# Token scatter inside the feed-forward phase, with the first weights loaded ahead of the wait

## The reference, cut to what matters

```python
x = x + _L0_ffn_ref(_layernorm(x)[None], ...)   # capacity: top 936 tokens by a score, one MLP (256 -> 1024 -> 256), gelu
x = x + _L1_ffn_ref(_layernorm(x)[None], ...)   # switch: each token to 1 of 8 experts (256 -> 1024 -> 256), relu
x = x + _L2_ffn_ref(_layernorm(x)[None], ...)   # top-2 of 8 experts, per-expert affine of the normed token, gelu
x = x + _L3_ffn_ref(_layernorm(x)[None], ...)   # top-2 of 16 experts (256 -> 512 -> 256), relu, residual, layernorm
...
buf = zeros(E, C, D).at[idx, pos_safe].set(x)   # tokens are put beside the others of their expert
y = relu(buf @ w1 + b1) @ w2 + b2               # one expert's weights for its tokens
out = gate * y[idx, pos]                        # and taken back by the token
```

## Time and profile before

| what | value |
|---|---|
| median of 3 runs | 4655.58 us (4652.52 to 4660.18) |
| profiled execution, its own time | 4685.71 us |
| span of that execution, first to last instruction | 4684.1 us |
| busy: PE, DVE, POOL, ACT | 2923.7, 2212.2, 1871.3, 867.9 us |
| mean granted TensorE clock | 0.778 |
| DMA, mean over the span | 128 GB/s |

### The profile page before, as it was taken

The page is one execution under the profiler, slowest core; times in us unless marked ns, Lnnn a source line. Parts: engine busy times, 40 slices in busy tenths (PEclk is TensorE's granted clock), DMA queues, the critical chain, the costliest instruction groups (busy, mean ns, idle before and its releaser), DMA issues. The chain is left out here.

```text
span 4684.1 us, 57224 instructions
## 1 busy us (share of the span) xinstructions
PE 2923.7 (62%) x16851; PEld 2401.0 (51%) x16852; DVE 2212.2 (47%) x5663; ACT 867.9 (19%) x2228; POOL 1871.3 (40%) x1982
## 2 busy tenths in 40 slices
PE   3566746664666566642568626665949639947392
PEld 3455535553555355522556413335938639936382
DVE  6655645554555555564243437681064421134113
ACT  1122312221222122210112100001300103310020
POOL 4366546664666466624323467731010020020212
PEclk7788878777887778875678657676979859978696
DMA  6633323332333233303312133315947449945594
GB/s 157 217 89 89 78 65 89 88 83 59 89 90 88 57 87 89 89 15 124 100 55 74 28 82 93 92 41 190 304 145 240 150 159 328 325 150 174 181 333 128
DMA packets 357397, 598.97 MB, mean 128 GB/s; under 512 B 81862, under 2 KB 239864, under 8 KB 354808
## 3 DMA queue, kind: packets, MB, share of 16 engines
q1 hardware_dynamic: 245816, 357.76, 23.3%
q0 software_dynamic: 88640, 214.25, 16.3%
q10 hardware_dynamic: 22656, 23.54, 1.5%
HBM read 499.63 MB, written 95.75 MB: 127 GB/s over the span
## 5 line engine op out<-in xcount | busy, mean ns | idle before, releaser
L833 POOL DMA_INDIRECT gine_got<-gine_table,src x1056 | 1024.5, 970 | 619.7 <-issue 251.1
L893 PE MATMUL gine_p_sum<-gine_hot,gine_got 128*128 128x128 f32 x4224 | 846.2, 334 | 565.1 <-DVE stack_acc L930 200.1
L893 PEld LDWEIGHTS gine_p_sum<-gine_hot,gine_got 128*128 128x128 f32 x4224 | 707.4, 238 | 719.0 <-issue 648.6
L922 DVE TENSOR_TENSOR gine_got<-gine_got,gine_p_edge 128x256 f32<-128x256 f32 x1056 | 440.2, 418 | 633.5 <-PE gine_p_edge L884 365.0
L901 ACT ACTIVATE gine_got<-gine_got 128x256 f32<-128x256 f32 x1056 | 439.0, 417 | 1201.1 <-issue 750.5
L488 POOL DMA_INDIRECT adjacency<-value,place x264 | 281.1, 1065 | 475.9 <-POOLq L54 166.2
L930 DVE TENSOR_TENSOR stack_acc<-stack_acc,gine_p_sum 128x256 f32 x1056 | 438.9, 416 | 3.5 <-issue 0.7
L883 PE MATMUL gine_p_edge<-gine_w_a,edge_space 128*128 128x256 bf16 x1056 | 338.3, 320 | 42.6 <-issue 34.7
L1368 PE MATMUL ffn_p_h<-ffn_xt,ffn_w 128*128 128x128 f32 x2864 | 347.3, 279 | 1.1 <-DMA ffn_w<-in_L_ffn_w 0.7
L1368 PEld LDWEIGHTS ffn_p_h<-ffn_xt,ffn_w 128*128 128x128 f32 x2864 | 337.3, 196 | 3.8 <-DMA ffn_w<-in_L_ffn_w 2.6
L884 PE MATMUL gine_p_edge<-gine_w_b,edge_space 128*128 128x256 bf16 x1056 | 336.8, 319 | 0.0
(11 more groups left out here) (398 smaller groups left out, 3526.2 us busy)
## 6 DMA issues: line engine op xcount, KB each, us to landing
gcn_a<-adjacency SPq DMA_DIRECT2D x270, 320.0 KB
ffn_w<-in_L_ffn_W SPq DMA_DIRECT2D x74, 1024.0 KB
ffn_w<-in_L_ffn_w SPq DMA_DIRECT2D x60, 1024.0 KB
ffn_w<-in_L_ffn_w SPq DMA_DIRECT2D x90, 512.0 KB
adjacency<-zero_row ACTq DMA_DIRECT2D x3, 7200.0 KB, 43.8
gine_got<-gine_table,src POOLq DMA_INDIRECT x1056
h_table<-score_rows SPq DMA_DIRECT2D x15, 1056.0 KB
adjacency<-zero_row SPq DMA_DIRECT2D x1, 7200.0 KB, 28.1
```

The lines of the kernel that those rows point to most:

```text
L833: pool.indirect_dma_start(got[:, c % RING, :], None, table, bass.IndirectOffsetOnAxis(ap=rows[:, c:c + 1], axis=0)).then_inc(gathered[c % ...
L893: ins = nc.tensor.matmul(p_sum[d % 4][:, half * P:(half + 1) * P], got[:, d % RING, half * P:(half + 1) * P], hot[:, d % HOTS, :], start=T ...
L922: nc.vector.tensor_tensor(got[:, c % RING, :], got[:, c % RING, :], p_edge[c % 4][:, 0:D], ALU.add).then_inc(summed, 1)
```

## The change

The phase `spread` is gone. Its scatters are now the first instructions of POOL in the block of `expert_blocks`, on a semaphore `placed`. SP issues w1(0), the vectors, w2(0) and w1(1), then waits for `placed`, and then issues x(0), x(1) and x(2). After that its loop goes on as before, without the loads that are already issued. The four callers pass the tokens (`rows`) in.

```diff
-def scatter_tokens(nc, g, rows, r, slots):
-    with Phase(nc, "spread") as ph:
-        sent = ph.sem("sent")
-        block = ph.block()
-        @block.gpsimd
-        def _(pool):
-            for k in range(r.choices):
-                for t in range(T):
-                    pool.indirect_dma_start(slots, bass.IndirectOffsetOnAxis(ap=r.slot[:, k, t:t + 1], axis=0),
-                                            rows[:, t, :], None).then_inc(sent, 16)
-            pool.wait_ge(sent, 16 * r.choices * T)
-
-def expert_blocks(nc, g, slots, results, r, w1, b1, w2, b2, func, affine=None):
+def expert_blocks(nc, g, rows, slots, results, r, w1, b1, w2, b2, func, affine=None):
...
-        small_in = ph.sem("small_in")
+        small_in, placed = ph.sem("small_in"), ph.sem("placed")
...
-            load_x(0)
             load_w1(0)
             sp.dma_start(b1_sb[:, :, :], b1.rearrange("a p m -> p a m")).then_inc(small_in, 16)
             sp.dma_start(b2_sb[:, :, :].rearrange("p a n -> p (a n)"), row(b2.rearrange("a n -> (a n)"))).then_inc(small_in, 16)
             if affine is not None:
                 for k in range(2):
                     sp.dma_start(aff[:, k, :, :], affine[k].rearrange("a p m -> p a m")).then_inc(small_in, 16)
-            for n in range(1, 3):
+            load_w2(0)
+            load_w1(1)
+            sp.wait_ge(placed, 16 * r.choices * T)
+            for n in range(3):
                 load_x(n)
             for n in range(1, nb + 1):
-                if n < nb:
+                if 1 < n < nb:
                     load_w1(n)
                 if n + 2 < nb:
                     load_x(n + 2)
-                load_w2(n - 1)
+                if n > 1:
+                    load_w2(n - 1)

         @block.gpsimd
         def _(pool):
+            for k in range(r.choices):
+                for t in range(T):
+                    pool.indirect_dma_start(slots, bass.IndirectOffsetOnAxis(ap=r.slot[:, k, t:t + 1], axis=0),
+                                            rows[:, t, :], None).then_inc(placed, 16)
             for n in range(nb):
                 pool.wait_ge(y_ready, n + 1)
...
-        scatter_tokens(nc, g, xn, r, slots)
-        expert_blocks(nc, g, slots, results, r, ...)
+        expert_blocks(nc, g, xn, slots, results, r, ...)
```

More of the change, by code:

```diff
@@ L1501, in capacity_ffn @@
         rank_tokens(nc, g, xn, i["L0_ffn_wr"].rearrange("d o -> (d o)"), i["L0_ffn_br"], chosen, r)
-        scatter_tokens(nc, g, xn, r, slots)
-        expert_blocks(nc, g, slots, results, r, i["L0_ffn_w1"].rearrange("(a d) f -> a d f", a=1), i["L0_ffn_b1"],
+        expert_blocks(nc, g, xn, slots, results, r, i["L0_ffn_w1"].rearrange("(a d) f -> a d f", a=1), i["L0_ffn_b1"],
                       i["L0_ffn_w2"].rearrange("(a d) f -> a d f", a=1), i["L0_ffn_b2"].rearrange("(a d) -> a d", a=1),
@@ L1523, in switch_ffn @@
         choose_experts(nc, g, xt, i["L1_ffn_gate_w"], i["L1_ffn_gate_b"], r, slots, capacity=capacity)
-        scatter_tokens(nc, g, xn, r, slots)
-        expert_blocks(nc, g, slots, results, r, i["L1_ffn_w1"], i["L1_ffn_b1"], i["L1_ffn_w2"], i["L1_ffn_b2"], ACT.Relu)
+        expert_blocks(nc, g, xn, slots, results, r, i["L1_ffn_w1"], i["L1_ffn_b1"], i["L1_ffn_w2"], i["L1_ffn_b2"], ACT.Relu)
         combine(nc, g, results, r.slot, r, g.X, guard=True)
@@ L1538, in top2_gelu_ffn @@
         layernorm(nc, g, xn, xn)
-        scatter_tokens(nc, g, xn, r, slots)
-        expert_blocks(nc, g, slots, results, r, i["L2_ffn_W1"], i["L2_ffn_b1"], i["L2_ffn_W2"], i["L2_ffn_b2"], ACT.Gelu,
+        expert_blocks(nc, g, xn, slots, results, r, i["L2_ffn_W1"], i["L2_ffn_b1"], i["L2_ffn_W2"], i["L2_ffn_b2"], ACT.Gelu,
                       affine=(i["L2_ffn_ln_g"], i["L2_ffn_ln_b"]))
@@ L1553, in top2_relu_ffn @@
         choose_experts(nc, g, xt, i["L3_ffn_gate_w"], i["L3_ffn_gate_b"], r, slots)
-        scatter_tokens(nc, g, xn, r, slots)
-        expert_blocks(nc, g, slots, results, r, i["L3_ffn_w1"], i["L3_ffn_b1"], i["L3_ffn_w2"], i["L3_ffn_b2"], ACT.Relu)
+        expert_blocks(nc, g, xn, slots, results, r, i["L3_ffn_w1"], i["L3_ffn_b1"], i["L3_ffn_w2"], i["L3_ffn_b2"], ACT.Relu)
         combine(nc, g, results, r.slot, r, xn)
```

## The result

| kernel | median | range, runs | ratio to before |
|---|---|---|---|
| before | 4655.0 us | 4652.52 to 4660.18, 6 | |
| after | 4621.18 us | 4618.93 to 4625.39, 6 | 0.9926 [0.9913, 0.9939] |

The change saves 34.4 us, [28, 40]; the forecast was 36.3 us and 4619.3 us. The profiled execution of after took 4619.35 us with a span of 4617.7 us and a mean granted clock of 0.779. Lines have moved: the scatter is L1337, x L1300, w1 L1306, w2 L1312, b1 L1315, b2 L1316, the affine vectors L1319, `turn` L1352, `up` L1360, `take` L1409 (with the affine L1412), the store L1341, the gather L1445.

The account below looks back on a forecast made before the run. POOL's own pace was taken to bound the scatter stretch, leaving only the wait behind it: 57.3 us before less 21.0 after saves 36.3, from the median 4655.6 to 4619.3 us. Own range 4613 to 4630, overall 4611 to 4633.

Parts of the forecast that it names:

- the chain: From the last scatter's end to `up`(0)'s start: 57.3 us over four places before, 21.0 after.
- x(0) to `up`(0): From x(0)'s issue to the first `up`: 8.2, 10.2, 11.6 and 12.5 us before, 3.4 after, 3.6 in `top2`.
- The landing of a scatter: From the last scatter's end to x(0)'s issue after the change: 1.8 us in all four places.
- the 1.2 us more with 30 scatters: Longer wait before x(0) in `top2` and `moe`, counted as part of the phase change, not of the landing.
- The loads are hidden: Early weights and vectors, 4.2 MB in `switch`, are done before the last scatter lands; nothing taken for them.
- the forecast's two cases: `switch`'s early loads: 13.5 us at 312 GB/s, or 18.0 us at 235 GB/s, a tie but still no loss.
- Rival A: Weight loads delay scatter landing and x(0): 11.2 us lost in all, 25.1 saved, 4630.5 us; chance 0.10.
- Rival C: POOL's scatters stall beside weight traffic, 3.93 us more each; three per place give 4666.5 us; chance 0.04.
- Rival B: Only the barrier between scatters and loads goes, the start-up stays: 7.6 us saved, 4648.0 us; chance 0.06.
- `up`(0): First `up` in each place: same times as before, 6.34, 5.13, 6.37 and 3.54 us.
- so the rest is shifted whole: From the end of `up`(0) on, same full buffers and same order in both kernels, so no further gain or loss.
- The barrier term: Barrier between last scatter and x(0) removed: 1.3, 1.3, 2.5 and 2.5 us, 7.6 saved in all.

Follow-up runs that it names:

- e2: The changed kernel with w2(0) and w1(1) issued behind x(0) to x(2), only w1(0) and the vectors ahead of the wait; 4334.48 us, ratio 0.9923 to before.
- e3: The changed kernel with the vectors b1, b2 and the affine issued behind x(0) to x(2), the weights still early; 4349.86 us, ratio 0.9971 to before.
- e4: The changed kernel with three more loads of 1 MB each ahead of SP's wait in each place; 4347.23 us, ratio 0.9957 to before.
- e1: The changed kernel with SP waiting for the scatters before its first load, then loading in the order of before; 4364.44 us against 4363.07, ratio 1.0006.
- e7: The changed kernel with 30 matmuls of no use on PE before turn(0), started at the sixth-last scatter's landing; 4649.9 us, ratio 0.9934 to before.
- e6: The kernel before with one scatter phase for each choice, so two phases of 15 scatters in `top2` and `moe`; 4664.45 us, run once.
- e5: The changed kernel with one POOL drain right behind its scatters; 4621.14 us, ratio 0.9922 to before.
- the change again: The changed kernel itself, unedited, run again as the base for other runs beside it; 4623.73 us, ratio 0.9930 to before.
- e9: The changed kernel without POOL's drain at the end of the four feed-forward blocks; 4617.55 us, ratio 0.9912 to before.
- e11: The changed kernel with POOL drains behind the scatters and each result store, none at the feed-forward blocks' ends; 4668.09 us, ratio 0.9967 to before.

## Why the prediction was right, and where not

- **What bounds the stretch.** Right. POOL's pace sets the scatter stretch (1.28 us, as before), and the only thing to be had was the chain behind it. e2 and e3 show the chain's parts one by one.
- **x(0) to `up`(0).** Forecast 3.4 us and 3.6 in `top2`; measured 3.44 to 3.50, and 3.74. This term carries the result: 28.5 of the 37.6 us. By e3 18.6 of them are the vectors.
- **The landing of a scatter.** Forecast 1.8 us from a gather's wait; 1.43 measured, in all four places. It was good for 1.5 us more than forecast. Right too was that the 1.2 us more with 30 scatters were not landing.
- **The loads are hidden.** Right, with DMA at 0.9 in the scatter stretch. In `switch` they took 17.4 us from SP's first issue and were done 1.7 us before the last scatter ended. That is near the worse of the forecast's two cases, 13.5 and 18.0, not the one it went by: 4.2 MB in 17.4 us are 241 GB/s, not 312. It was made good in part by the start, 0.25 us before the first scatter where the forecast had 0.8 after it. Rival A did not happen, but in `switch` it is near. e4 shows what it is like: SP waits 3.6 and 3.4 us more, nearly all of it for the scatters' own data. Rival A's price, 3.2 us for one weight load, was not measured: e4 adds three.
- **Rival C.** No scatter's instruction stalled: 1.02 us at most in after, and the pace held in e4 beside full DMA engines. But the instruction is not the whole scatter: in e4 the data came 3 us late at an unchanged pace, which the argument from the 539 ns of a store could not see.
- **Rival B.** e1 is this rival built: only the barrier goes. The forecast gave it 7.6 us; it saved nothing that the medians show.
- **`up`(0).** The sum was forecast unchanged at 21.4 and is 20.9, with single ones off by up to 1.5 us either way. e7 shows that the clock at 0.50 is what makes them long.
- **The step that failed** is "so the rest is shifted whole". The forecast put the 1.2 us more with 30 scatters down to "the phase change", as if they went away with it. But the cost goes with the scatters (e6), 15 of them bear it as well, and they moved into a block that has an end of its own (e1, e5): 90 scatters at 0.083 us are 7.5 us. The barrier term was 9.2 us saved in front and 7.5 paid behind, net 1.7, instead of 7.6. With the 1.5 us more from the landing already in the 9.2, the forecast of 36.3 should have been 30.6. The measured 34.4 [28, 40] holds both, and the change again gave 32.5. So that the forecast came within 2 us of the median is in part luck: by the trace it was 5.7 us too high, and the medians can't tell the two apart.

## What to carry to other kernels

Work that one phase leaves to its end is moved, not removed, when the phase is merged into the next: before counting a barrier as saved, look at the wait at the end of the block that inherits the instructions. Loads that need nothing of the running phase, above all large vectors spread over the partitions, belong in front of its wait, as long as they are done before the last scatter is: beside them POOL's instructions keep their pace, but the data fall behind. A drain of POOL costs nothing once, where POOL idles anyway, but repeated behind every store it waits for each store's data and can set the pace of a stage.

## What the runs showed of the hardware that was not expected

- The drain at the end of a block costs POOL 0.083 to 0.086 us for each DMA that it issued in the block, scatter or plain store (e9: 23, 37, 67 and 75 DMAs cost 1.97, 3.12, 5.59 and 6.24 us). One drain in an idle stretch takes this off the path (e5); without a drain at the end it comes back at the next one (e9: 5.6 us in `moe`, 5.0 in `top2`). What POOL does in this time no row names.
- A scatter's semaphore reaches a waiting SP 1.43 us after the end of POOL's instruction with the DMA engines otherwise idle, and 5.04 and 4.79 us after it with weights in flight (e4), while POOL's own pace of 1.28 us doesn't change. Of the difference (3.6 and 3.4 us) 3.3 and 3.0 us are the scatters' own data, written late.
- Right behind a single store a drain held POOL until 0.9 to 1.2 us after the store's last packet (1.6 once), some 5 us in all beside full DMA engines (e11, `moe`).
- The granted clock rose from 0.50 to 1.00 between 2179 and 2183 us while PE was busy throughout (e7), and `up`(0) fell to 3.81 us, near the 3.74 of those behind it.
